# Three stores of a query and a key block instead of six stores of one block

## What is computed

```python
qkv = x @ W_attn + b_attn                        # x: (2, 2048, 256)
scores = einsum('bhtd,bhsd->bhts', q, k) * 16 ** -0.5
mask = (j <= i) & (j >= i - 64)
x = layernorm(x + softmax(where(mask, scores, -inf)) @ v @ W_proj + b_proj)
expert = argmax(softmax(x @ Wr.T))               # one of 8 for each token
inter = gelu(x @ W1[expert] + b1[expert])        # 256 -> 1024
y = inter @ Wo + bo + x
x = layernorm(x + layernorm(y) * gamma + beta)
```

## Time and profile before

| | |
|---|---|
| time, median of 3 runs | 568.05 us (567.16 to 576.44) |
| span of the profiled execution | 569.7 us |
| PE busy | 505.2 us, 89% |
| DVE busy | 413.9 us, 73% |
| ACT busy | 354.5 us, 62% |
| POOL busy | 320.2 us, 56% |
| stores of `qk_hi` | 64 of 128 KB, 2.7 us from issue to landing |
| stores of `qk_lo` | 32 of 128 KB, 3.3 us |
| DMA packets | 95048, 75.34 MB |

### The profile page before, as it was taken

The page is one execution under the profiler, slowest core; times in us unless marked ns, Lnnn a source line. Parts: engine busy times, 40 slices in busy tenths (PEclk is TensorE's granted clock), DMA queues, the critical chain, the costliest instruction groups (busy, mean ns, idle before and its releaser), DMA issues. The chain is left out here.

```text
span 569.7 us, 24810 instructions
## 1 busy us (share of the span) xinstructions
PE 505.2 (89%) x8591; PEld 444.1 (78%) x8591; DVE 413.9 (73%) x1100; ACT 354.5 (62%) x800; POOL 320.2 (56%) x570
## 2 busy tenths in 40 slices
PE   4599899989999999999977549999999999999980
PEld 3478788878787888888865439999999999998870
DVE  3746777787787977778766535888888888886443
ACT  2455667757677677776766327666666677664550
POOL 7702244535454454544455523888888888885433
PEclk9899899999999999999999659999999999999996
DMA  9597676676767887767662021333322222221000
GB/s 204 147 201 216 153 211 184 184 218 179 212 174 205 221 227 205 205 187 210 174 180 72 20 75 40 95 96 104 84 70 76 73 81 67 78 67 50 25 10 7
DMA packets 95048, 75.34 MB, mean 132 GB/s; under 512 B 37190, under 2 KB 88527, under 8 KB 94930
## 3 DMA queue, kind: packets, MB, share of 16 engines
q1 hardware_dynamic: 91570, 65.31, 43.6%
q0 software_dynamic: 3264, 8.41, 4.3%
q10 hardware_dynamic: 96, 0.04, 0.0%
HBM read 43.63 MB, written 23.62 MB: 118 GB/s over the span
## 5 line engine op out<-in xcount | busy, mean ns | idle before, releaser
L1416 PE MATMUL ps<-v_even,w_hi 128*128 128x128 f16 (+1 forms) x1280 | 170.5, 215 | 1.8 <-issue 1.1
L1416 PE MATMUL ps<-v_even,w_lo 128*128 128x128 f16 (+1 forms) x640 | 132.2, 214 | 0.0
L837 ACT ACTIVATE probs<-ps,b1T 128x128 f32<-128x128 f32 (+1 forms) x320 | 87.0, 360 | 72.5 <-PE ps L1416 54.1
L1398 PE MATMUL ps<-wo_hi,ks 128*128 128x256 f16 x576 | 128.6, 273 | 1.0 <-DVE ks L1087 1.0
L1416 PEld LDWEIGHTS ps<-v_even,w_hi 128*128 x1280 | 120.9, 98 | 7.4 <-issue 3.7
L870 DVE TENSOR_REDUCE mx<-ps 128x4 bf16<-128x512 f32 x128 | 83.4, 683 | 20.9 <-PE ps L1195 13.6
L629 POOL CAST att_hi<-att 128x256 f16<-128x256 f32 x32 | 12.7, 396 | 120.9 <-DVE att L928 120.9
L1398 PE MATMUL ps<-wo_lo,ks 128*128 128x256 f16 x288 | 78.5, 273 | 0.0
L734 ACT ACTIVATE probs<-ps 128x512 f32<-128x512 f32 x128 | 69.8, 611 | 9.9 <-PE ps L1221 7.5
L1244 PE MATMUL ps<-v_even,probs 128*64 128x17 f32 x1024 | 71.6, 210 | 3.8 <-issue 3.0
L1244 PE MATMUL ps<-v_odd,probs 128*64 128x17 f32 x1024 | 71.8, 210 | 3.5 <-issue 3.4
(11 more groups left out here) (225 smaller groups left out, 1254.1 us busy)
## 6 DMA issues: line engine op xcount, KB each, us to landing
qk_s<-qk_hi SPq DMA_DIRECT2D x64, 128.0 KB, 2.7
w_in<-in_L_ffn_W_dram SPq DMA_DIRECT2D x32, 256.0 KB, 3.0
v_odd<-slots SPq DMA_DIRECT2D x64, 128.0 KB
qs<-qk_s SPq DMA_DIRECT2D x16, 384.0 KB
ks<-qk_s SPq DMA_DIRECT2D x16, 384.0 KB, 4.9
ks<-qk_s SPq DMA_DIRECT2D x32, 144.0 KB, 3.7
v_even<-v_odd SPq DMA_DIRECT2D x63, 68.0 KB, 3.4
qk_s<-qk_lo SPq DMA_DIRECT2D x32, 128.0 KB, 3.3
```

Of the source, the lines that this page charges most:

```text
L837: last = nc.scalar.activation(g[1 - p][:, ic, n * width:(n + 1) * width], ps_h[1 - p][:, half, col + n * width:col + (n + 1) * width], ACT ...
L1398: ins = mm(ps_y[p], h[p][hs][:, ic, :], wo[ws][:, ic, :], start=n == 0, stop=n == 3 * IC - 1)
L1416: up_ins = mm(ps_h[1 - p][:, half, col + m * width:col + (m + 1) * width], weights(ws, owners[m], k, ic), sT[1 - p][ss][:, k, at], start=k ...
```

## The change

The scratch tensor `qk_s` gets another order: a pair's query and key block now lie one behind the other. A new function `terms` describes, as one access, one term of the query block and one term of the key block. So one transfer writes a part's 256 KB: for each of 128 channels 1 KB of queries and 1 KB of keys. Per pair there are three: high to terms (0, 0), high to terms (1, 2), low to terms (2, 1). The waits before them are the same, and the loads read the same bytes from their new places. `QK_STORES` is 3.

```diff
--- before.py
+++ after.py
@@ -74,8 +74,14 @@
     w1_units = w1.rearrange("e (k p) i -> (e k) p i", p=P)
     slots = nc.dram_tensor("slots", [SLOTS, ROW], f32, kind="Internal").ap()
 
-    qk_s = nc.dram_tensor("qk_s", [2, TILES // 2, P, 3, CC, 2 * P], f16, kind="Internal").ap()
-    PARTS = ((0, 0, 1), (0, 1, 0))
+    PIECE = CC * 2 * P
+    qk_s = nc.dram_tensor("qk_s", [TILES // 2, 2, P, 3, PIECE], f16, kind="Internal").ap()
+
+    def terms(g, q_term, k_term):
+
+        block = P * 3 * PIECE
+        return bass.AP(qk_s.tensor, 2 * g * block + q_term * PIECE,
+                       [[3 * PIECE, P], [block + (k_term - q_term) * PIECE, 2], [1, PIECE]])
 
     def wait(eng, sem, count):
         if not isinstance(count, int) or count > 0:
@@ -324,7 +330,7 @@
         out_st = [sem(f"out_st{k}") for k in range(2)]
 
         QK_LOADS, ATTN_LOADS, SMALL_LOADS, FFN_LOADS = 2, 3, 2, 3
-        QK_STORES, ROW_STORES = 6, 3
+        QK_STORES, ROW_STORES = 3, 3
         N_CONSTS = 1
 
         def apart(eng):
@@ -411,7 +417,7 @@
 
             def stack_sources(g):
 
-                return (qk_s[w, g].rearrange("(h d) j m n -> (d j) h m n", d=HD) for w in range(2))
+                return (qk_s[g, w].rearrange("(h d) j (m n) -> (d j) h m n", d=HD, m=CC) for w in range(2))
 
             def windows(g, m, new, landing):
 
@@ -419,7 +425,7 @@
                 dst = ks[k][0:ALIGNED:2, 0, :, :].rearrange("r (h m) n -> r h m n", m=CC)[:, :, m, :]
                 sp.dma_start(dst[:, :, BLK:2 * P], new[:, :, m, 0:2 * P - BLK]).then_inc(landing, 16)
                 if g > 0:
-                    prev = qk_s[1, g - 1].rearrange("(h d) j m n -> (d j) h m n", d=HD)
+                    prev = qk_s[g - 1, 1].rearrange("(h d) j (m n) -> (d j) h m n", d=HD, m=CC)
                     sp.dma_start(dst[:, :, 0:BLK], prev[:, :, m, 2 * P - BLK:2 * P]).then_inc(landing, 16)
 
             def stacks_begin(g):
@@ -483,14 +489,12 @@
                 n = it + LEAD
                 if n % 2 == 1 and a_tile(n):
                     g = n // 2
-                    for part in range(2):
-                        sp.wait_ge(qkl_done if part else qkh_done, n + 1)
-                        for w in range(2):
-                            for term in range(3):
-                                if PARTS[w][term] == part:
-                                    sp.dma_start(qk_s[w, g, :, term, :, :].rearrange("p m n -> p (m n)"),
-                                                 qk[g % 2][part][:, w, :, :].rearrange("p m n -> p (m n)"))\
-                                        .then_inc(qk_st[g % 2], 16)
+                    hi, lo = (part[:, :, :, :].rearrange("p w m n -> p w (m n)") for part in qk[g % 2])
+                    sp.wait_ge(qkh_done, n + 1)
+                    sp.dma_start(terms(g, 0, 0), hi).then_inc(qk_st[g % 2], 16)
+                    sp.dma_start(terms(g, 1, 2), hi).then_inc(qk_st[g % 2], 16)
+                    sp.wait_ge(qkl_done, n + 1)
+                    sp.dma_start(terms(g, 2, 1), lo).then_inc(qk_st[g % 2], 16)
 
             sp.wait_ge(slots_known, 1)
             for k in range(ROWS):
```

## The result

The changed kernel took 558.49 us at the median (557.65 to 569.88, 4 runs), the kernel before 567.67 us (567.16 to 576.44, 4 runs). The ratio is 0.9833 with an interval of 0.9813 to 0.9853, that is 9.2 us less. The forecast was 567.4 us with a range down to 563.8, so it missed. Medians in this document are over all executions of a kernel; the ratios leave out disturbed ones, which ran longer at a lower granted clock.

The account below looks back on a forecast made before the run. PE's own work was taken to bound the attention stage. Only 0.7 us of PE's 0.84 us of waits at pair 1 would come back, so 568.05 - 0.7 = 567.35, rounded 567.4 us, with a range of 563.8 to 571.5 us.

Parts of the forecast that it names:

- What bounds the kernel: Attention stage: PE's own work sets the pace; a DMA change pays only where PE waits, 1.0 us on ks loads.
- The 2.4 us of slack: Pair 2: its last ks load is there at 69.3 us, the scores run at 71.79, so an earlier load changes nothing.
- Issues: SP's queue: six old stores take 2.7 us to issue, three new 1.3 to 1.8; SP gains 0.9 to 1.4 per pair.
- Landing 0.4 us earlier in an ordinary pair: DMA engines need 2.3 us for a pair's data against 2.7 of issuing, so the last store lands 0.4 us earlier.
- Pair 0 and pair 1: Start of the stage: pair 0's stores land 0.7 us earlier, bounds 0 and 1.4; everything up to 52 us moves up.
- PE's waits on ks near 0.2 us: Sign of being right: PE's waits on the loads that read the stored data fall from 1.0 to near 0.2 us.
- SP's wait on `w_lo` longer: Sign of being right: SP's queue waits 0.5 to 1 us more per pair for DVE, up to 60 us in all.
- The 0.84 us: Pair 1: PE's two waits for ks loads, 0.53 and 0.31 us, the most to be had; 0.7 us comes back.
- The sum: Whole kernel: median 568.05 us less 0.7 gives 567.35, rounded 567.4 us; the profiled execution of 569.7 would give 569.0.
- Rival (b): PE's instruction fetches, 16 KB blocks over the same DMA engines, fall better: 563.9 us, or 557 at most; chance 0.14.
- (e): Faster by over 2%: fixed cost paid per transfer, every pair's chain on the path; 47 us less, 521 us; chance 0.01.
- (d): Slower by over 2%: the new store form streams slowly, each pair's loads come late; 33 us more, 601; chance 0.02.

Follow-up runs that it names:

- the shifted ones: Kernel before, with POOL's two scattered stores of rows issued one step later, in odd instead of even steps of POOL's loop: 584.54 us, ratio 1.014.
- The same program: Changed kernel with the 256 KB load of w1 in odd steps issued behind the three stores: 556.23 us on chip 7, 567.55 us on chip 13.

## Why the prediction was wrong

*What bounds the kernel.* Right: PE sets the pace of the stage. The waits on the ks loads were taken from one profile, 1.0 us, as a property of the kernel. They differ by core: on those without the hold the kernel before waits 4.1 and 5.7 us for them, and the stop shown above cost almost three times its length through the clock. The 2.4 us of slack that hid an ordinary pair were read in a profile in which the hold made PE late.

*Issues.* Right for the new form: three take about 1.5 us per pair (0.5 was taken for one). Too low for the old: 2.7 us for six is six times the median issue, but the queue holds single ones (up to 1403 ns in the earlier trace rows), and at the median of the pairs six took 3.1 to 3.7 us in the profiles of the kernel before. So SP gains about 2 us per pair, where at most 1.4 was taken. In the changed kernel's profile the first and the last form:

```profile
L494 SPq DMA_DIRECT2D qk_s<-qk_hi x16: 386/434/1606, 15.1 to 271.3; - x16
...
L497 SPq DMA_DIRECT2D qk_s<-qk_lo x16: 465/556/1931, 16.2 to 272.4; - x16
```

*Landing 0.4 us earlier in an ordinary pair, bounds 0 and 1.4.* Within its bounds: the load that waits for the landing starts 0.5 to 1.1 us earlier after the mark (first profiles and chips 7 and 8). Each store of the low part alone is later from issue to landing, 4.8 us instead of 3.3, which passes the "much over 3.5 us" that was named as a sign of being wrong. SP's wait for the last store grew from 16.2 to 30.9 us between 30 and 315 us, about 1 us per pair; about half of what issuing saved turned into waiting.

*Pair 0 and pair 1.* The follow-up of pair 0 was to go near 22.0 us and went at 18.93, that of pair 1 near 40.9 and went at 37.72. The stretch from pair 0's first store to that load shrank from 5.32 to 3.78 us, 1.5 where 0.7 was taken (its upper bound was 1.4). This is not one number of the kernel either: the stretch is 4.1, 5.4 and 5.5 us in the changed kernel on chips 7, 6 and 8, and 5.9 and 6.3 us in the kernel before on 7 and 8. The rest is an earlier start of the whole stage, which other executions of the kernel before show as well (first store at 14.56 and 14.81 us).

```profile
15.15 0.39 SPq L494 DMA_DIRECT2D qk_s<-qk_hi  x1
...
16.20 0.51 SPq L497 DMA_DIRECT2D qk_s<-qk_lo  x1
18.93 0.58 SPq L436 DMA_DIRECT2D qs<-qk_s  x1
```

*PE's waits on ks near 0.2 us, SP's wait on w_lo longer.* Neither shows in the two first profiles: 1.2 us in one wait, and 43.7 us against 45.8. Side by side on one chip both moved as forecast: PE's waits on ks fell by 2.8 us (chip 8) and 1.8 us (chip 7), and SP's wait on `w_lo` grew from 40.2 to 50.6 and from 37.2 to 49.1 us, 0.7 us per pair. The 0.84 us that were "the most that can be had" were too little for these cores.

*The sum.* The step that failed is the base of the sum, 568.05 us, from which 0.7 was taken as if a second measurement elsewhere would have the same base, with only "a little for the spread of the times" in the range. The base itself moves by 6 to 10 us between chips: the unchanged kernel took 573.7 to 575.1 us on chips with the hold, 565.6 to 567.5 us on those without, and the changed one 572.61 us on chip 6 and 562.18 on chip 7. The sum also read the profiled span of 569.7 us as a time, 1.65 us above the median; as a time it is about 571.4, so that profile, with its hold, was of a slower execution than the base.

Beside a kernel before on the same chip the change is worth 2.5, 2.7 and 4.7 us by the medians on chips 6, 8 and 7, and by the ratios 0.998 (0.994 to 1.003), 0.993 (0.988 to 0.997) and 0.988 (0.983 to 0.993), that is 0.9, 4.2 and 7.0 us. On chip 6, with the hold, that is not told from nothing, and three stores in the old layout gave 0.999 there. On chips 8 and 7 the intervals lie below 1, but so did that of an unchanged copy (0.992, 0.985 to 1.000). So from nothing to a little over 1% is all that can be said of the change's size. For a gain on cores without the hold speak the shorter waits on ks on both; it is likely and not shown. Whether 0.7 us was right as the change's own worth can't be said either. What of the 9.2 us lies above the change's worth was luck, that of the cores or moments of two measurements; how it divides between the hold and other causes was not measured.

*The rivals.* The last sentence of the prediction said that several microseconds should be found in PE's "issue" stops and the clock behind them. The place was right in part: L1248's stops fell from 6.4 to 0.5 us, and the step with the stop of 1.8 us from 11.60 to 8.13 us. That the change does it was not. Rival (b) blamed PE's instruction fetches, 16 KB blocks falling better; but most of the short stops come in every second step behind POOL's scattered stores, on some cores, in whatever kernel, and the long one is absent from the unchanged kernel on chips 7 and 8 too (steps of 8.12 and 8.13 us). Whether a fetch made it was not tested. For (e) and the rule to coalesce of the Trainium skill, *DMA: Bandwidth & Descriptors*, "Rules for kernel authors": the runs give it part of its due, 0.5 to 1.1 us per pair and not 6. In "Anatomy of one DMA" of the same page the Trainium skill gives the 2.0 us behind the 6 for transfers issued from GpSimd, and these stores are SP's. The slow side is real too: (d) put slower by over 2% down to a burst that takes 3.2 us more, and twelve stores, whose load goes some 4.5 us later, showed such a cliff at 59 us.

**What stays open.** What a core with the hold has that another has not; and since the core is not on record, even whether it is the core, the chip or the moment. The hold goes with POOL's scattered stores (the shifted ones moved it), it is not in the order of buffers, and doubling the stores does not make it on a core without it. Whether the number of stores scales it where it exists was not tried, as no such run fell on a chip with the hold. The first measurement of the changed kernel shows a core without the hold and the profile of before one with it; that the two came from different cores is concluded from the later runs. The hold does not explain every base: the first three times of the kernel before that agree, 567.16 to 568.05 us, lie among those of chips without the hold. A difference between cores of another kind is known: the Trainium skill, *DMA: Bandwidth & Descriptors*, "iDMA fabric — 4 AXI ports for 8 engines, asymmetric across TPBs", reports that full-rate reads of HBM by POOL's cores through their own DMA path hinder the load stream of one core of a pair and not that of the other, in measurements that it calls unchecked. No run here tells which core of a pair it ran on, the scattered stores are not such reads, and here it is PE's signals that are late.

## What to carry to other kernels

Before a difference of 1 or 2% is explained, run the kernel before again beside the changed one, see that the profile is of an execution as long as those timed, and compare one wait group or step length in both: a base that differs by core is seen at once, and a cause found by comparing two profiles alone can be the core's. A slack read from one profile holds for that core; where the engine that bounds is faster elsewhere, the transfer hidden behind it becomes the path. For a round trip through DRAM, count from the event that starts it to the load that ends it, and look at what is queued in front of the stores: moving a 256 KB load behind them gained 4.2 us with six stores (chip 13), at least as clearly as halving their number did, and 6 us on top of the halving (chip 7).

## What the runs showed of the hardware

- The same program takes 567.55 us on one core and 556.23 us on another, at nearly the same mean granted clock in their profiles (0.946 and 0.953). Of the 14.6 us between the two profiles 7.6 are in twelve steps, mostly 8.9 against 8.13 us, in which POOL issues scattered stores.
- A stop of 1.6 us of PE for a load was followed by a granted clock of 0.50 in the stretch from 119 to 123 us, and its step took 5.2 us longer. A stop of 1.07 us was followed by 0.54 and 0.60 in one profile, one of 1.08 us at the same place by 1.00 in another.
- Twelve stores of 64 partitions and 64 KB instead of six of 128 and 128 KB, the same bytes, cost 59 us at the median; three of 256 KB gained from nothing to a little over 1%.
